# Transposing the normalised input by DMA instead of on TensorE

## Chip, cores and metric

One NeuronCore of a Trainium2 chip runs the whole program; all float32 inputs and the float32 output lie in HBM. The metric is device time in microseconds (us), the median of several runs. The cores of such a chip have five engines: TensorE (PE, matrix products into PSUM), VectorE (DVE), ScalarE (ACT), GpSimd (POOL) and SyncE (SP), which here only issues DMAs.

## What is computed

The input is x of shape (4, 2048, 512), four sequences. The reference, cut to what matters:

```python
xn  = layernorm(x)                                   # over 512 columns, no gain or bias
q,k,v = heads(xn @ Wq.T + bq), ...                   # 64 heads of 8
q,k = softmax(exp(beta) * q), softmax(exp(beta) * k) # within a head
num = einsum(q, cumsum(k v)); den = sum(q * cumsum(k))   # causal linear attention
attn = (num / den) @ Wo.T + bo
ffn  = fp8_round(clip(xn / input_scale)) @ (weight_fp8 * weight_scale).T + bias
out  = x + attn + ffn
```

## The kernel before

The 2048 positions are cut into 64 steps of 32 positions; a step takes them from all four sequences, so it is a tile of 128 rows (partitions) by 512 columns. Step i is spread over several bodies: body i of every engine holds the projections of step i, the causal scores, the state and the attention sums of step i - 1, and the output projection, the fp8 part and the final sum of step i - 2. Each engine has its own instruction stream with its own `body(i)`; nothing but hand-placed semaphore waits orders them. What an engine is given later in its own stream can't overtake what stands ahead of it.

The input of step i + 1 is prepared within body i. In the kernel before:

- DVE normalises it near the start of its body (`normalise`, L556, writes xn, L561), after a_n of step i - 2 and before `shift` of step i takes k_max and k_shift from the K bank (L594, L598).
- PE transposes xn late in its body (`input_transpose`, L834 to L839, four float32 128x128 transposes into the PSUM bank t_ps), between the output projection (L817 to L819) and the state part of the attention sums (L941).
- ACT reads t_ps twice (`high_input`, L409 to L418): xh, the float16 high part, and y, the value to be rounded to fp8. It does so behind q_heads (L464).
- DVE takes the low part, xl = t_ps - xh (`low_input`, L570), then y_exp and y_magic (`magic`, L575, L580), all after o_sb of step i - 2 (L704), then vp of step i (L713), which waits for PE's V projection of step i, and last xq, the clipped rounded value (`quantise`, L588).
- POOL adds and takes away y_magic (`rounding`, L357, L361), which rounds, and then adds the bias to the residual x_res (L373).

PE's body starts with the K projection of step i (`project`, L806 to L810: per 128-row chunk xh by w_hi, xh by w_lo, xl by w_hi, twelve matmuls), which waits for xh and xl of that step and for the bank's seed. Its V projection waits for o_sb of step i - 2, for it uses the same bank; it ends the body together with the last attention sums (L955).

The reciprocal standard deviations are made for two steps at a time, only in bodies with an even i: DVE computes the two variances and a first guess (`variances`, L542 to L554) near the end of its body, behind `statistics` of step i + 3; POOL refines the guess with three Newton rounds (`root`, L330 to L351, twelve small dependent operations). In POOL's body of an even i `root(i + 2)` stands first, ahead of `rounding(i + 1)` (L365 to L368). DVE's `quantise(i + 1)` waits for that rounding. Below, an even body that has these is called a root step, the others plain steps.

SP's body loads x of step i + 4 once xn of step i + 1 has been made, stores o_sb of step i - 2 and loads x_res of step i. DVE, ACT and POOL take all bodies from 4 to 59 in a loop of four; so did SP.

Of the kernel before, what the change touches and what calls it, by code (L numbers as in the profile page):

```python
# [31 lines left out]
P = 128  # L32
# [87 lines left out]
def build(nc, x, wq, bq, wk, bk, wv, bv, wo, bo, beta, wf, bf, in_scale, w_scale, const, out):  # L120
# [3 lines left out]
    with ExitStack() as ctx:  # L124
# [46 lines left out]
        xn = sb("xn", [P, DM])  # L171
        xh = sb("xh", [P, 2, KC, P], F16)
        xl = sb("xl", [P, 2, KC, P], F16)
        y = sb("y", [P, DM])
# [66 lines left out]
        newton_steps = sem("newton_steps")  # L241
        xn_ready, xT_done, xh_ready, xl_ready = sem("xn_ready"), sem("xT_done"), sem("xh_ready"), sem("xl_ready")
        y_ready, yexp_ready, magic_ready = sem("y_ready"), sem("yexp_ready"), sem("magic_ready")
# [47 lines left out]
        @block.sync  # L291
        def _(sp):
            def load_x(t):
                if t.after(SLOTS):
                    sp.wait_ge(xn_ready, (t - SLOTS + 1).n)
                sp.dma_start(x_in[:, t.slot, :], x_t[t.n]).then_inc(x_loaded[t.slot], 16)

            def body(i):
                if (i + SLOTS).exists():
                    load_x(i + SLOTS)  # L300
                t = i - 2
                if t.exists():
                    sp.wait_ge(o_ready, (t + 1).n)
                    sp.dma_start(out_t[t.n], o_sb[:, t.parity, :]).then_inc(stored[t.parity], 16)
                if i.exists():
                    sp.dma_start(x_res[:, i.parity, :], x_t[i.n]).then_inc(r_loaded[i.parity], 16)

            for n, s in enumerate((beta, in_scale, w_scale)):
                sp.dma_start(scal[:, n:n + 1], s.rearrange("(a n) -> a n", a=1).to_broadcast([P, 1]))\
                    .then_inc(m_loaded, 16)  # L310
            for t in range(PAIR):
                load_x(Step(0, t))
            sp.dma_start(cst[:, :], const).then_inc(c_loaded, 16)
            for m in turn:
                sp.dma_start(w_nat[m][:, :, :], weights[m].rearrange("(c p) d -> p c d", p=P))\
                    .then_inc(w_loaded[m], 16)
            for t in range(PAIR, SLOTS):
                load_x(Step(0, t))
            iterations(sp, body)
            for n in range(2):  # L320
                sp.wait_ge(stored[n], 16 * (STEPS // 2))
# [3 lines left out]
        def _(pool):  # L325
# [4 lines left out]
            def root(t):  # L330
# [5 lines left out]
                for n in range(NEWTON):  # L336
# [14 lines left out]
                    r = nxt  # L351

            def rounding(t):

                pool.wait_ge(y_ready, (t + 1).n)
                pool.wait_ge(magic_ready, (t + 1).n)
                gp.tensor_tensor(y_sum[:, :], y[:, :], y_magic[:, :], ALU.add).then_inc(ysum_ready, 1)  # L357
                pool.wait_ge(ysum_ready, (t + 1).n)
                if t.after(1):
                    pool.wait_ge(xq_ready, t.n)  # L360
                gp.tensor_tensor(y_round[:, :], y_sum[:, :], y_magic[:, :], ALU.subtract)\  # L361
                    .then_inc(yround_ready, 1)

            def body(i):
                if i.parity == 0 and (i + PAIR).exists():  # L365
                    root(i + PAIR)
                if (i + 1).exists():
                    rounding(i + 1)  # L368
                t = i - 1
# [5 lines left out]

            root(Step(0, 0))
            rounding(Step(0, 0))
            pool.wait_ge(amax_ready, 3)
# [24 lines left out]
        def _(act):  # L403
# [5 lines left out]
            def high_input(t):  # L409

                act.wait_ge(xT_done, (t + 1).n)
                if t.after(2):
                    act.wait_ge(v_done, (t - 1).n)
                sc.activation(flat(xh[:, t.parity]), t_ps[:, :], ACT.Copy).then_inc(xh_ready, 1)
                if t.after(1):
                    act.wait_ge(ysum_ready, t.n)
                    act.wait_ge(magic_ready, t.n)
                sc.activation(y[:, :], t_ps[:, :], ACT.Copy, scale=in_inv[:, :]).then_inc(y_ready, 1)  # L418

            def body(i, last_weights=None, fold=False):  # L420
                t = i - 1
                if t.exists():
# [4 lines left out]
                    for b in range(SEQS):  # L427
                        last = sc.activation(v_seqs[:, t.parity, :, b, :], vp[:, t.parity, :, :],  # L428
                                             ACT.Copy, scale=seq_mask[:, b:b + 1])
                    last.then_inc(vseqs_ready, 1)  # L430
                if i.exists():
                    act.wait_ge(kshift_ready, (i + 1).n)
# [18 lines left out]
                if i.exists():  # L451
# [14 lines left out]
                    last.then_inc(qheads_ready, 1)  # L466
                if (i + 1).exists():
                    high_input(i + 1)
                t = i - 1
# [50 lines left out]
        def _(dve):  # L520
# [35 lines left out]
            def normalise(t):  # L556

                dve.wait_ge(rstd_ready, (t + PAIR).half)
                if t.after(1):
                    dve.wait_ge(xT_done, t.n)  # L560
                v.tensor_scalar(xn[:, :], x_in[:, t.slot, :], mv[:, t.slot, 0:1],  # L561
                                rstd[:, t.slot:t.slot + 1], ALU.subtract, ALU.mult).then_inc(xn_ready, 1)

            def low_input(t):

                dve.wait_ge(xh_ready, (t + 1).n)
                dve.wait_ge(y_ready, (t + 1).n)
                if t.after(2):
                    dve.wait_ge(v_done, (t - 1).n)
                v.tensor_tensor(flat(xl[:, t.parity]), t_ps[:, :], flat(xh[:, t.parity]), ALU.subtract)\  # L570
                    .then_inc(xl_ready, 1)

            def magic(t):

                v.tensor_scalar(y_exp[:, :].bitcast(I32), y[:, :].bitcast(I32), EXPONENT, None,  # L575
                                ALU.bitwise_and).then_inc(yexp_ready, 1)
# [6 lines left out]
            def quantise(t):  # L583

                dve.wait_ge(yround_ready, (t + 1).n)
                if t.after(SLOTS):
                    dve.wait_ge(f_done, (t - SLOTS + 1).n)
                v.tensor_scalar(flat(xq[:, t.slot]), y_round[:, :], FP8_MAX, -FP8_MAX, ALU.min, ALU.max)\  # L588
                    .then_inc(xq_ready, 1)
# [38 lines left out]
            def body(i, last_weights=None, fold=False):  # L628
# [38 lines left out]
                if i.exists():  # L667
# [4 lines left out]
                    if i.after(2):  # L672
# [4 lines left out]
                        .then_inc(kT_ready, 1)  # L677
                    shift(i, q_ps, q_done, q_max, qmax_ready, q_shift, qshift_ready, qe_ready)
                t = i - 1
                if t.exists():  # L680
# [26 lines left out]
                if t.exists():  # L707
                    low_input(t)
                    magic(t)
                if i.exists():  # L710
# [4 lines left out]
                        .then_inc(vp_ready, 1)  # L715
                if t.exists():
                    quantise(t)

# [40 lines left out]
            largest(MQ)  # L759
            low_input(Step(0, 0))  # L760
            magic(Step(0, 0))
# [33 lines left out]
        def _(pe):  # L795
# [7 lines left out]
            def project(bank, t, m, seeded):  # L803

                for c in range(KC):
                    mm(bank[:, :], xh[:, t.parity, c, :], w_hi[:, m, c, :], start=(c == 0 and not seeded),  # L806
                       stop=False, skip_group_check=seeded)
                    mm(bank[:, :], xh[:, t.parity, c, :], w_lo[:, m, c, :], start=False, stop=False,  # L808
                       skip_group_check=seeded)
                    last = mm(bank[:, :], xl[:, t.parity, c, :], w_hi[:, m, c, :], start=False,  # L810
                              stop=(c == KC - 1), skip_group_check=seeded)
# [21 lines left out]

            def input_transpose(t):  # L834

                pe.wait_ge(xn_ready, (t + 1).n)
                for c in range(KC):
                    last = transpose(t_ps[:, P * c:P * (c + 1)], xn[:, P * c:P * (c + 1)], ident)
                last.then_inc(xT_done, 1)  # L839

            def body(i, low_part=True, last_weights=None, fold=False):
                if i.exists():
                    pe.wait_ge(xh_ready, (i + 1).n)
                    pe.wait_ge(xl_ready, (i + 1).n)
                    pe.wait_ge(kseed_ready, (i + 1).n)
# [10 lines left out]
                if t.exists():  # L856
                    pe.wait_ge(an_ready, (t + 1).n)
                    if i.exists():
                        pe.wait_ge(y_ready, (i + 1).n)
                    for b in range(SEQS):  # L860
# [3 lines left out]
                if fold:  # L864
                    pe.wait_ge(bias_ready, 3)
                    pe.wait_ge(y_ready, (i + 1).n)
                    for j in range(J):
# [22 lines left out]
                if t.exists():  # L890
                    pe.wait_ge(xq_ready, (t + 1).n)
                    if (t + 1).exists():
# [30 lines left out]
                if (i + 1).exists():  # L923
                    if fold:
                        pe.wait_ge(bvl_ready, 1)
                    else:
                        pe.wait_ge(xl_ready, (i + 1).n)
                        pe.wait_ge(y_ready, (i + 1).n)
                    input_transpose(i + 1)
                t = i - 1  # L930
# [48 lines left out]
            pe.wait_ge(c_loaded, 16)  # L979
            input_transpose(Step(0, 0))  # L980
            for m in (MK, MQ, MV):
# [45 lines left out]
```

## Time and profile before

| | us |
|---|---|
| runs of the kernel before | 1460.99, 1455.46, 1458.12 (median 1458.12) |
| the profiled execution | 1454.77 |
| its span, first to last instruction | 1452.9 |

| engine | busy us | share of the span |
|---|---|---|
| PE | 1328.5 | 91% |
| DVE | 1130.3 | 78% |
| ACT | 704.8 | 49% |
| POOL | 333.6 | 23% |

Busy time counts each instruction from its start to its modelled end; matmuls overlap, so PE's share is not a share of its peak. The DMA engines moved 61.83 MB, a mean of 43 GB/s. The granted TensorE clock was 0.985 of full speed over the span. The steady part runs from about 105 us to the end.

### The profile page before, as it was taken

How to read it: one execution, taken by the hardware profiler on the slowest of the kernel's cores; microseconds unless marked ns; L12 is line 12 of the kernel's file. 1: busy time of each engine (PE TensorE's matmuls, PEld its weight loads, DVE VectorE, ACT ScalarE, POOL GpSimd, SP SyncE). 2: the span in 40 equal slices, each digit the busy share in tenths (PEclk: the TensorE clock that was granted, in tenths of full speed). 3: DMA queues.
4: the chain of work that ended last, by engine and by line, in shares of the span. 5: the costliest groups of instructions: out<-in, count | busy, mean ns of one | idle time of the engine just before them, and what ended most of it. 6: DMA issues, size and time to landing. Idle time of an engine off the chain costs nothing.

```text
span 1452.9 us, 81228 instructions
## 1 busy us (share of the span) xinstructions
PE 1328.5 (91%) x36578; PEld 827.2 (57%) x36578; DVE 1130.3 (78%) x2095; ACT 704.8 (49%) x1241; POOL 333.6 (23%) x588
## 2 busy tenths in 40 slices
PE   1679999999999999999999999999999999999996
PEld 1345655655565555565556556556565655555664
DVE  3667877877787787787788778788778877877873
ACT  0554455545545544554554544555455455445542
POOL 1122222122222212212212222221222222122120
PEclk9699999999999999999999999999999999999999
DMA  7001111111111111111111111111111111111011
GB/s 216 25 10 28 45 47 33 39 46 40 33 46 46 30 42 47 33 39 47 36 36 46 43 30 46 47 34 38 47 40 32 46 46 31 41 46 34 24 33 33
DMA packets 29583, 61.83 MB, mean 43 GB/s; under 512 B 1377, under 2 KB 1505, under 8 KB 29281
## 3 DMA queue, kind: packets, MB, share of 16 engines
q1 hardware_dynamic: 28560, 55.67, 12.7%
q8 instruction: 291, 4.77, 1.4%
q10 hardware_dynamic: 720, 1.31, 0.4%
q14 instruction: 12, 0.09, 0.0%
HBM read 40.20 MB, written 16.78 MB: 39 GB/s over the span
## 4 chain that ended last, share of the span: by engine, by line
PE 33%; DVE 24%; issue 24%; POOL 11%; ACT 5%; DMA 1%; POOLq 1%; DVEq 0%; SPq 0%; ACTq 0%
PE s_ps L829 7%; POOL y_sum L357 3%; DVE st_step L612 3%; POOL y_round L361 3%; DVE att L623 3%; PE a_ps L955 2%; PE a_ps L915 2%; PE k_ps L806 2%; PE vo_ps L897 2%; DVE st_masked L606 2%; PE vo_ps L806 2%; PE k_ps L808 2%; PE k_ps L810 2%; DVE stats L536 2%; PE vo_ps L808 1%
## 5 line engine op out<-in xcount | busy, mean ns | idle before, releaser
L428 ACT ACTIVATE v_seqs<-vp,cst 128x576 f32<-128x576 f32 x256 | 184.8, 799 | 185.7 <-DVE vp L713 185.7
L829 PE MATMUL s_ps<-q_heads,kT 32*32 32x128 f32 x8192 | 249.7, 269 | 0.0
L829 PEld LDWEIGHTS s_ps<-q_heads,kT 32*32 32x32 f32 x8192 | 215.3, 105 | 53.7 <-issue 53.6
L357 POOL TENSOR_TENSOR y_sum<-y,y_magic 128x512 f32<-128x512 f32 x64 | 81.7, 1276 | 524.9 <-DVE y_magic L580 524.9
L464 ACT ACTIVATE q_heads<-qT,cst 128x512 f32<-128x512 f32 x256 | 164.1, 713 | 38.8 <-DVE qT L687 38.8
L623 DVE TENSOR_TENSOR att<-s_ps,cst 128x512 f32<-128x512 f32 x256 | 163.8, 681 | 0.2 <-PE s_ps L829 0.2
L455 ACT ACTIVATE q_e<-q_shift,q_exp_scale 128x512 f32<-128x512 f32 x64 | 46.3, 723 | 242.0 <-DVE q_shift L598 242.0
L588 DVE TENSOR_SCALAR xq<-y_round 128x512 f16<-128x512 f32 x64 | 92.0, 1437 | 80.4 <-POOL y_round L361 80.1
L436 ACT ACTIVATE k_e<-k_shift,k_exp_scale 128x512 f32<-128x512 f32 x64 | 46.3, 724 | 192.8 <-DVE k_shift L598 192.8
L806 PE MATMUL vo_ps<-w_hi,xh 128*128 128x512 f16 x256 | 97.7, 382 | 31.4 <-DVE o_sb L704 30.4
L713 DVE TENSOR_TENSOR vp<-vo_ps,vp 128x512 f32<-128x512 f32 x64 | 44.3, 692 | 102.6 <-PE vo_ps L810 102.6
L343 POOL TENSOR_TENSOR newton<-guess 128x2 f32<-128x2 f32 x32 | 6.2, 195 | 476.8 <-DVE guess L553 470.0
L806 PE MATMUL k_ps<-w_hi,xh 128*128 128x512 f16 x256 | 99.4, 388 | 12.2 <-issue 8.3
L941 PE MATMUL a_ps<-st_seqs,q_heads 128*32 128x36 f32 x8192 | 88.5, 201 | 20.0 <-issue 19.3
L817 PE MATMUL vo_ps<-w_hi,ah 128*128 128x512 f16 x260 | 99.5, 383 | 0.8 <-issue 0.8
L818 PE MATMUL vo_ps<-w_lo,ah 128*128 128x512 f16 x260 | 98.8, 380 | 0.7 <-issue 0.7
L808 PE MATMUL k_ps<-w_lo,xh 128*128 128x512 f16 x256 | 98.7, 385 | 0.6 <-issue 0.6
L819 PE MATMUL vo_ps<-w_hi,al 128*128 128x512 f16 x260 | 98.7, 380 | 0.2 <-issue 0.2
L810 PE MATMUL k_ps<-w_hi,xl 128*128 128x512 f16 x256 | 98.4, 384 | 0.0
L941 PEld LDWEIGHTS a_ps<-st_seqs,q_heads 128*32 128x32 f32 x8192 | 78.7, 109 | 33.6 <-issue 33.0
L955 PEld LDWEIGHTS a_ps<-v_seqs,att 128*32 128x32 f32 x8192 | 78.0, 109 | 33.7 <-issue 33.6
L808 PE MATMUL vo_ps<-w_lo,xh 128*128 128x512 f16 x256 | 97.0, 379 | 0.0
(138 smaller groups left out, 2648.5 us busy)
## 6 DMA issues: line engine op xcount, KB each, us to landing
x_in<-L_attn_x SPq DMA_DIRECT2D x64, 256.0 KB
x_res<-L_attn_x SPq DMA_DIRECT2D x64, 256.0 KB
out<-o_sb SPq DMA_DIRECT2D x64, 256.0 KB
w_own<-L_attn_Wk SPq DMA_DIRECT2D x1, 1024.0 KB, 12.4
w_own<-L_attn_Wq SPq DMA_DIRECT2D x1, 1024.0 KB, 14.4
w_own<-L_attn_Wv SPq DMA_DIRECT2D x1, 1024.0 KB, 16.2
att<-L_ffn_weight_fp SPq DMA_DIRECT2D x1, 1024.0 KB, 17.8
v_seqs<-L_attn_Wo SPq DMA_DIRECT2D x1, 1024.0 KB, 15.3
```

Of the source, the lines that this page charges most:

```text
L357: gp.tensor_tensor(y_sum[:, :], y[:, :], y_magic[:, :], ALU.add).then_inc(ysum_ready, 1)
L428: last = sc.activation(v_seqs[:, t.parity, :, b, :], vp[:, t.parity, :, :], ACT.Copy, scale=seq_mask[:, b:b + 1])
L464: last = sc.activation(q_heads[:, i.parity, :, j, :], qT[:, :, :], ACT.Copy, scale=head_mask[:, j:j + 1])
L623: v.tensor_tensor(att[:, 4 * c:4 * c + 4, :, :].rearrange("p g j s -> p (g j) s"), s_ps[:, DM * (c % 2):DM * (c % 2 + 1)].rearrange("p (h ...
L806: mm(bank[:, :], xh[:, t.parity, c, :], w_hi[:, m, c, :], start=(c == 0 and not seeded), stop=False, skip_group_check=seeded)
L808: mm(bank[:, :], xh[:, t.parity, c, :], w_lo[:, m, c, :], start=False, stop=False, skip_group_check=seeded)
L810: last = mm(bank[:, :], xl[:, t.parity, c, :], w_hi[:, m, c, :], start=False, stop=(c == KC - 1), skip_group_check=seeded)
L817: mm(vo_ps[:, :], ah[:, j, :], w_hi[:, MO, j, :], start=(j == 0 and not rest), stop=False)
L818: mm(vo_ps[:, :], ah[:, j, :], w_lo[:, MO, j, :], start=False, stop=False)
L829: last = mm(s_ps[rows, DM * (c % 2) + P * gg:DM * (c % 2) + P * (gg + 1)], kT[rows, t.parity, g, :], q_heads[rows, t.parity, g, :, :], sta ...
L941: mm(a_ps[TOK * j:TOK * (j + 1), a_col(g):a_col(g) + GW], q_heads[:, t.parity, g, j, :], st_seqs[:, t.parity, g, :, :], start=(g % (G // 2 ...
L955: last = mm(a_ps[TOK * j:TOK * (j + 1), a_col(g):a_col(g) + GW], att[:, g, j, :], v_seqs[:, t.parity, J * g + j, :, :], start=False, stop= ...
```

## The change

xn is no longer transposed on PE. ACT writes the float16 high part of xn in the natural layout into one half of a new tile x_split, POOL writes the low part into the other half (`low_input` is now POOL's), and SP transposes both halves with one DMA (`dma_start_transpose`, 128x1024 float16) into xT, of which there are two. y and the fp8 rounding are in the natural layout too; DVE writes xq_rows (one buffer), and SP transposes it (128x512 float16) into xq.

Order on the engines: ACT's `high_input(i + 1)` moves to the front of the body, behind v_seqs and ahead of k_e. DVE's `magic(i + 1)` moves ahead of the second pair of score masks (L623), `quantise(i + 1)` ahead of vp, and `low_input` leaves DVE. POOL runs `low_input(i + 1)` between `root(i + 2)` and `rounding(i + 1)`. SP issues both transposes behind the load of x and ahead of the store of o_sb and the load of x_res; its bodies are written out instead of looped. PE waits for x_turned in place of xh and xl, and for xq_turned in place of xq. The transposes of a_n now wait for al of the step before (L659) in place of y. The diff, cut:

```diff
 SP
+            def turn_x(t):
+                sp.wait_ge(xl_ready, (t + 1).n)
+                if t.after(2):
+                    sp.wait_ge(v_done, (t - 1).n)
+                sp.dma_start_transpose(xT[:, t.parity].rearrange("p h c s -> p (h c) s"),
+                                       x_split[:, :, :].rearrange("p h d -> p (h d)")).then_inc(x_turned, 16)
+                sp.wait_ge(xq_ready, (t + 1).n)
+                if t.after(SLOTS):
+                    sp.wait_ge(f_done, (t - SLOTS + 1).n)
+                sp.dma_start_transpose(xq[:, t.slot, :, :], xq_rows[:, :]).then_inc(xq_turned, 16)
             def body(i):
                 if (i + SLOTS).exists():
                     load_x(i + SLOTS)
+                if (i + 1).exists():
+                    turn_x(i + 1)
 POOL
+            def low_input(t):
+                pool.wait_ge(xh_ready, (t + 1).n)
+                gp.tensor_tensor(x_split[:, 1, :], xn[:, :], x_split[:, 0, :], ALU.subtract)\
+                    .then_inc(xl_ready, 1)
                 if i.parity == 0 and (i + PAIR).exists():
                     root(i + PAIR)
                 if (i + 1).exists():
+                    low_input(i + 1)
                     rounding(i + 1)
 ACT, high_input(t), now behind v_seqs in body(i)
-                act.wait_ge(xT_done, (t + 1).n)
-                if t.after(2):
-                    act.wait_ge(v_done, (t - 1).n)
-                sc.activation(flat(xh[:, t.parity]), t_ps[:, :], ACT.Copy).then_inc(xh_ready, 1)
+                act.wait_ge(xn_ready, (t + 1).n)
+                if t.after(1):
+                    act.wait_ge(x_turned, t.n * 16)
+                sc.activation(x_split[:, 0, :], xn[:, :], ACT.Copy).then_inc(xh_ready, 1)
-                sc.activation(y[:, :], t_ps[:, :], ACT.Copy, scale=in_inv[:, :]).then_inc(y_ready, 1)
+                sc.activation(y[:, :], xn[:, :], ACT.Copy, scale=in_inv[:, :]).then_inc(y_ready, 1)
 DVE
             def normalise(t):
-                    dve.wait_ge(xT_done, t.n)
+                    dve.wait_ge(xl_ready, t.n)
+                    dve.wait_ge(y_ready, t.n)
                     shift(i, q_ps, q_done, q_max, qmax_ready, q_shift, qshift_ready, qe_ready)
+                if (i + 1).exists():
+                    magic(i + 1)
                 t = i + 1
                 if t.exists():
-                    low_input(t)
-                    magic(t)
+                    quantise(t)
                 if i.exists():
                     dve.wait_ge(v_done, (i + 1).n)
                     ...                               # vp
-                if t.exists():
-                    quantise(t)
 DVE, quantise(t)
-                if t.after(SLOTS):
-                    dve.wait_ge(f_done, (t - SLOTS + 1).n)
-                v.tensor_scalar(flat(xq[:, t.slot]), y_round[:, :], FP8_MAX, -FP8_MAX, ALU.min, ALU.max)\
+                if t.after(1):
+                    dve.wait_ge(xq_turned, t.n * 16)
+                v.tensor_scalar(xq_rows[:, :], y_round[:, :], FP8_MAX, -FP8_MAX, ALU.min, ALU.max)\
 PE
-                    pe.wait_ge(xh_ready, (i + 1).n)
-                    pe.wait_ge(xl_ready, (i + 1).n)
+                    pe.wait_ge(x_turned, (i + 1).n * 16)
-                    if i.exists():
-                        pe.wait_ge(y_ready, (i + 1).n)
+                    if t.after(1):
+                        pe.wait_ge(al_ready, t.n)
-                    pe.wait_ge(xq_ready, (t + 1).n)
+                    pe.wait_ge(xq_turned, (t + 1).n * 16)
-                if (i + 1).exists():
-                    ...
-                    input_transpose(i + 1)
```

## Rows read from the trace of the kernel before

**Rows 1.** The page: busy time of each engine, and its share of the span.
```profile
PE 1328.5 (91%) x36578; PEld 827.2 (57%) x36578; DVE 1130.3 (78%) x2095; ACT 704.8 (49%) x1241; POOL 333.6 (23%) x588
```
**Rows 2.** Timeline of DVE: start, length, line, operation [idle before, releaser].
```profile
704.93 0.68 DVE L594 TENSOR_REDUCE k_max<-k_ps 128x64 f32<-128x512 f32 x1
...
717.81 0.17 DVE L553 TENSOR_SCALAR guess<-shifted 128x2 int32<-128x2 int32 x1
717.98 0.75 DVE L704 SCALAR_TENSOR_TENSOR o_sb<-vo_ps,out_dn,x_res 128x512 f32<-128x512 f32 x1
...
721.59 0.69 DVE L713 TENSOR_TENSOR vp<-vo_ps,vp 128x512 f32<-128x512 f32 x1 [1.47 <-PE vo_ps L810]
724.18 1.49 DVE L588 TENSOR_SCALAR xq<-y_round 128x512 f16<-128x512 f32 x1 [1.89 <-POOL y_round L361]
725.59 0.56 DVE L635 RECIPROCAL den_rec<-a_ps 128x32 f32<-128x32 f32 x2
...
727.30 0.69 DVE L594 TENSOR_REDUCE k_max<-k_ps 128x64 f32<-128x512 f32 x1
...
739.31 0.75 DVE L704 SCALAR_TENSOR_TENSOR o_sb<-vo_ps,out_dn,x_res 128x512 f32<-128x512 f32 x1
...
747.46 0.68 DVE L594 TENSOR_REDUCE k_max<-k_ps 128x64 f32<-128x512 f32 x1
```
**Rows 3.** All of k_max in the trace: least, median, longest ns, first and last start.
```profile
L594 DVE TENSOR_REDUCE k_max<-k_ps x64: 681/686/694, 58.0 to 1407.8; 128x64 f32<-128x512 f32 x64
```
**Rows 4.** Timeline of POOL in the root step of Rows 2.
```profile
718.06 0.20 POOL L343 TENSOR_TENSOR newton<-guess 128x2 f32<-128x2 f32 x1 [15.04 <-DVE guess L553]
...
721.36 0.20 POOL L349 TENSOR_TENSOR rstd<-newton 128x2 f32<-128x2 f32 x1
721.51 1.29 POOL L357 TENSOR_TENSOR y_sum<-y,y_magic 128x512 f32<-128x512 f32 x1
722.88 1.27 POOL L361 TENSOR_TENSOR y_round<-y_sum,y_magic 128x512 f32<-128x512 f32 x1
724.10 1.28 POOL L373 TENSOR_TENSOR x_res<-x_res,bias 128x512 f32<-128x512 f32 x1
```
**Rows 5.** Timeline of PE over the same two steps; only first matmuls of groups.
```profile
716.55 0.60 PE L838 MATMUL t_ps<-cst,xn 128*128 128x128 f32 x4
717.08 1.31 PE L941 MATMUL a_ps<-st_seqs,q_heads 128*32 128x36 f32 x128
...
722.73 0.39 PE L806 MATMUL k_ps<-w_hi,xh 128*128 128x512 f16 x1
...
725.42 1.95 PE L829 MATMUL s_ps<-q_heads,kT 32*32 32x128 f32 x64
...
740.12 0.39 PE L806 MATMUL vo_ps<-w_hi,xh 128*128 128x512 f16 x1 [1.08 <-DVE o_sb L704]
...
744.05 0.39 PE L806 MATMUL k_ps<-w_hi,xh 128*128 128x512 f16 x1
```
**Rows 6.** Groups by line: busy us, mean ns, idle before and its releaser.
```profile
L580 DVE TENSOR_SCALAR y_magic<-y_exp 128x512 f32<-128x512 f32 x64 | 27.3, 427 | 2.2
L575 DVE TENSOR_SCALAR y_exp<-y 128x512 int32<-128x512 int32 x64 | 26.8, 419 | 0.0
L343 POOL TENSOR_TENSOR newton<-guess 128x2 f32<-128x2 f32 x32 | 6.2, 195 | 476.8 <-DVE guess L553 470.0 <-issue 6.8
```
**Rows 7.** DMA issues of the start: size, median us from issue to landing.
```profile
scal<-L_attn_beta SPq DMA_DIRECT2D x1, 0.5 KB, 2.6
bias<-L_attn_bq ACTq DMA_DIRECT2D x1, 256.0 KB, 4.5
w_own<-L_attn_Wk SPq DMA_DIRECT2D x1, 1024.0 KB, 12.4
```
**Rows 8.** Stretches of PE in body 1: length, busy, granted clock; and its timeline.
```profile
74.00:76.00 2.00, 0.00 (x0) 0.70 0.00 0
```
```profile
78.47 0.58 PE L806 MATMUL k_ps<-w_hi,xh 128*128 128x512 f16 x1 [7.46 <-issue]
...
82.69 1.95 PE L829 MATMUL s_ps<-q_heads,kT 32*32 32x128 f32 x64
```

More of the change, by code:

```diff
@@ L171, in build @@
         xn = sb("xn", [P, DM])
-        xh = sb("xh", [P, 2, KC, P], F16)
-        xl = sb("xl", [P, 2, KC, P], F16)
+        x_split = sb("x_split", [P, 2, DM], F16)
+        xT = sb("xT", [P, 2, 2, KC, P], F16)
+        xq_rows = sb("xq_rows", [P, DM], F16)
         y = sb("y", [P, DM])
@@ L241, in build @@
         newton_steps = sem("newton_steps")
-        xn_ready, xT_done, xh_ready, xl_ready = sem("xn_ready"), sem("xT_done"), sem("xh_ready"), sem("xl_ready")
+        xn_ready, xh_ready, xl_ready = sem("xn_ready"), sem("xh_ready"), sem("xl_ready")
+        x_turned, xq_turned = sem("x_turned"), sem("xq_turned")
         y_ready, yexp_ready, magic_ready = sem("y_ready"), sem("yexp_ready"), sem("magic_ready")
@@ L318, in _ @@
                 load_x(Step(0, t))
-            iterations(sp, body)
+            turn_x(Step(0, 0))
+            for i in range(STEPS + 2):
+                body(Step(0, i))
             for n in range(2):
@@ L376, in _ @@
             root(Step(0, 0))
+            low_input(Step(0, 0))
             rounding(Step(0, 0))
@@ L430, in body @@
                     last.then_inc(vseqs_ready, 1)
+                if (i + 1).exists():
+                    high_input(i + 1)
                 if i.exists():
@@ L466, in body @@
                     last.then_inc(qheads_ready, 1)
-                if (i + 1).exists():
-                    high_input(i + 1)
                 t = i - 1
@@ L559, in normalise, with magic @@
                 if t.after(1):
-                    dve.wait_ge(xT_done, t.n)
+                    dve.wait_ge(xl_ready, t.n)
+                    dve.wait_ge(y_ready, t.n)
                 v.tensor_scalar(xn[:, :], x_in[:, t.slot, :], mv[:, t.slot, 0:1],
                                 rstd[:, t.slot:t.slot + 1], ALU.subtract, ALU.mult).then_inc(xn_ready, 1)
-            def low_input(t):
-                dve.wait_ge(xh_ready, (t + 1).n)
+            def magic(t):
                 dve.wait_ge(y_ready, (t + 1).n)
[L568 to L573, printed above, removed]
                 v.tensor_scalar(y_exp[:, :].bitcast(I32), y[:, :].bitcast(I32), EXPONENT, None,
@@ L678, in body @@
                     shift(i, q_ps, q_done, q_max, qmax_ready, q_shift, qshift_ready, qe_ready)
+                if (i + 1).exists():
+                    magic(i + 1)
                 t = i - 1
@@ L759, in _ @@
             largest(MQ)
-            low_input(Step(0, 0))
             magic(Step(0, 0))
@@ L805, in project @@
                 for c in range(KC):
-                    mm(bank[:, :], xh[:, t.parity, c, :], w_hi[:, m, c, :], start=(c == 0 and not seeded),
+                    mm(bank[:, :], xT[:, t.parity, 0, c, :], w_hi[:, m, c, :], start=(c == 0 and not seeded),
                        stop=False, skip_group_check=seeded)
-                    mm(bank[:, :], xh[:, t.parity, c, :], w_lo[:, m, c, :], start=False, stop=False,
+                    mm(bank[:, :], xT[:, t.parity, 0, c, :], w_lo[:, m, c, :], start=False, stop=False,
                        skip_group_check=seeded)
-                    last = mm(bank[:, :], xl[:, t.parity, c, :], w_hi[:, m, c, :], start=False,
+                    last = mm(bank[:, :], xT[:, t.parity, 1, c, :], w_hi[:, m, c, :], start=False,
                               stop=(c == KC - 1), skip_group_check=seeded)
@@ L832, in scores @@
                 last.then_inc(scores_done, 1)
[L834 to L839, printed above, removed]
             def body(i, low_part=True, last_weights=None, fold=False):
                 if i.exists():
-                    pe.wait_ge(xh_ready, (i + 1).n)
-                    pe.wait_ge(xl_ready, (i + 1).n)
+                    pe.wait_ge(x_turned, (i + 1).n * 16)
                     pe.wait_ge(kseed_ready, (i + 1).n)
@@ L857, in body @@
                     pe.wait_ge(an_ready, (t + 1).n)
-                    if i.exists():
-                        pe.wait_ge(y_ready, (i + 1).n)
+                    if t.after(1):
+                        pe.wait_ge(al_ready, t.n)
+                    else:
+                        pe.wait_ge(bvl_ready, 1)
                     for b in range(SEQS):
@@ L865, in body @@
                     pe.wait_ge(bias_ready, 3)
-                    pe.wait_ge(y_ready, (i + 1).n)
                     for j in range(J):
@@ L979, in _ @@
             pe.wait_ge(c_loaded, 16)
-            input_transpose(Step(0, 0))
             for m in (MK, MQ, MV):
```

6 lines of the change are left out of this document (removed).

## The prediction

> **What bounds the kernel now.** The page's busy times [rows 1] make PE look like the bound at 91%. Two views next to each other correct that. The DVE timeline gives the pace: k_max, one per step, starts at 704.93, 727.30 and 747.46 [rows 2], so a root step takes 22.37 us and a plain step 20.16 us, 42.53 for the pair. Over the trace, 63 intervals from 58.0 to 1407.8 us make 21.4 us each [rows 3], the same half pair, so what holds for one pair holds for the kernel. Newton rounds start 32 times [rows 6]; one is ahead of the loop, so 31 bodies are root steps.
>
> Why is a root step 2.2 us longer? DVE's guess ends at 717.98, POOL's Newton chain runs from 718.06 to 721.56, y_sum and y_round follow from 721.51 to 724.15 [rows 4], and DVE's xq waits 1.89 us for y_round; only then come den_rec and the next k_max [rows 2]. So the chain guess, Newton, rounding, xq sets the length of a root step. PE starts its next K projection at 722.73 and is done by 725.42 [rows 5], 1.9 us before DVE takes k_max: PE is not late there. In the plain step DVE runs nearly without a stop from k_max (727.30) to the end of o_sb (740.06), V starts at 740.12 having waited 1.08 us for it [rows 5], and the period closes through xq again. There both engines are near their limits.
>
> One more thing is in these rows. xq takes 1.49 us, y_magic, the same kind of operation, 0.43 [rows 6]. xq starts at 724.18, just behind the start of POOL's x_res (724.10 to 725.38) [rows 4]; it ends just after it.
>
> **The change, part by part.**
>
> *PE* loses four transposes: 716.55 to 717.08, 0.53 us a step [rows 5], 34 us over 64 steps. This is worth something only where PE is the late one, which it isn't in a root step.
>
> *DVE* loses xl (0.60 us), which lay in the wait for the V projection, where there is 1.47 us of idle time besides. That gain is nothing. y_exp and y_magic (0.42 + 0.43 = 0.85 us [rows 6]) come out of that same cover and go into the stretch between k_max and o_sb, which has no slack. So o_sb, and in a root step the guess too, come 0.85 us later. xq moves into the wait for V. In a plain step that takes it off the path, and away from x_res: it should take about 0.43.
>
> *Plain step after:* k_max to the end of o_sb 12.76 + 0.85 = 13.61. Then 0.06, then V, the last attention sums and K: 740.12 to 744.05 is 3.93, and K is 2.69 long (722.73 to 725.42) [rows 5]. Sum 20.3 against 20.16. The xq path gave room but o_sb, V, K close in its place: no gain, + 0.15 us.
>
> *Root step after,* counted from k_max (704.93 = 0). POOL's order is root(i + 2), low_input(i + 1), rounding(i + 1). So the low part of the next step's input, which DVE used to make at 718.65 without asking POOL, now stands behind the Newton chain:
> - guess ends at 13.05 + 0.85 = 13.90;
> - Newton 3.50 + 0.08 (717.98 to 721.56): 17.48;
> - low_input on POOL, two inputs 128x512, nearest row y_sum, 1.29 [rows 4]: 18.8;
> - the DMA transpose of 256 KB, issue to landing: D, below;
> - K of the next step 2.69, then k_max.
>
> D is in no row: no DMA transposes here. The lower bound is the 0.5 KB load, 2.6 us from issue to landing, the upper the 1 MB load of 12.4 us (which had two loads beside it) [rows 7]. Nearest in size is the first bias row, 256 KB, 4.5 us; I take that. With 0.1 us for the waits on both sides K starts at 23.4 and ends at 26.1.
>
> The Trainium skill has two rules that disagree here. "Advanced Engine Details and Errata", section X-Bar Transpose (TRN2), says transpose DMAs are as fast as regular ones, which goes with the 4.5 us row. "VectorE: DVE Perf Modes", The three transpose paths, gives 1309 ns for one 128x128 block by DMA against 390 on TensorE, which speaks against the change; one after the other, eight blocks would be an estimate of 10.5 us, and the total about 1810. No row decides between them.
>
> The clock. PE's last work before that K ends 13.90 + 0.75 (o_sb) + 0.06 + 3.93 = 18.65. So PE would be idle for 4.8 us in every root step. The trace has such a case in body 1: idle from about 71 us, the granted clock fell within 74 to 76 us, and the K projection after it took 78.47 to 82.69 = 4.22 us in place of 2.69 [rows 8]. That is 1.2 for 2.4 GHz through most of it: + 1.53. K ends at 27.6, and the root step is 27.6 against 22.37: + 5.25.
>
> *The other path of a root step,* which K hides by then: rounding behind low_input ends at 18.8 + 2.64 = 21.45; xq beside x_res as now 1.41 (724.18 to 725.59); vp, now behind xq, 0.69; den_rec to k_max 1.71 [rows 2]. Sum 25.3. So a root step can't be under 25.3 whatever D is: quantise now stands ahead of vp and takes it along. This is the floor: + 2.9.
>
> *The rest at nothing.* In a plain step low_input follows xn and xh at the start of the body, some 6 us after PE's K start, and K of the next step is 20 us behind K: even D = 12.4 is hidden, if by 1 or 2 us only. ACT's two operations move ahead of k_e; ACT waits for k_shift there now, and its early place is free as long as v_seqs (started by vp) is out of the way, which holds where K is the late one. The transpose of xq has two bodies before PE reads it. SP waits for xq_ready in mid-body with the store of o_sb, the load of x_res and the next load of x behind it; the first two used to wait for o_sb, which ends 8 us earlier in a root step and 0.5 in a plain one, and x_res has a whole body until POOL adds it, the load of x four. If that cover went, a late x_res would hold o_sb and so V, us for us. Body 0 has a root step too; I charge it like the others.
>
> **Sum.** 31 x 5.25 = 163, 31 x 0.15 = 5. On the profiled execution's 1454.8 that gives 1623 us. It lies 3.4 us (0.2%) under the median of the runs, which I leave inside the range.
>
> **Rivals.**
>
> 1. *The clock stays up.* PE idles under 2 us at a time in the steady part now and keeps its clock; at 4.8 us the fall in body 1 speaks for a loss. Without it: 31 x 3.7 + 5 = 120, 1575 us.
> 2. *Rounding decides, not the transpose.* If D is under 3.7 us, K ends before 25.3 and the xq, vp path closes the step: 31 x 2.9 + 5 = 95, 1550 us. For it: the 0.5 KB load lands in 2.6 us, and the source is on the chip. Against: 256 KB took 4.5.
> 3. *Slow transposes.* With D = 12.4, K ends at 18.8 + 12.5 + 2.69 + 1.53 = 35.5: 31 x 13.1 + 5 = 412, 1867 us. For it: nothing in the trace moves two-byte elements from one partition to another, so the row I took may be of the wrong kind. Against: the DMA engines are almost idle in this trace (43 GB/s).
> 4. *Faster.* The mechanism: xq under the V projection, and four transposes fewer. It decides if neither path behind Newton is late, that is if K's path and xq's path of a root step both stay under 22.37, for which D would have to be under 0.9 us and the rounding 2.9 us earlier. Then a root step would close like a plain one, with 0.6 us for variances: 20.9, and the pair 41.2 in place of 42.5: 31 x 1.3 = 40, 1414 us. Against it stand POOL's order and the rows of the Newton chain.
>
> **Chances.** Forecast (root step closed by a transpose of 3.7 to 8 us, clock lost) 0.42; the same with the clock kept 0.15; rounding decides 0.15; slow transposes, over 8 us, 0.19; faster 0.05; the parts cancel within 0.5% (what a measurement of this kernel can tell from no change) 0.04. Faster by over 0.5% 0.05, same 0.04, slower 0.91. The range: the low end is the floor of the root step, 1550. The far end of D, 1867, stands for the last tenth of the chances; I stop at 1810, where D would be 10.5, so that about 2 in 10 lie outside in all.
>
> **What the profile of after would show.** Right: k_max intervals that alternate near 20.3 and 25 to 28; K's first matmul in root steps waiting for x_turned, released by the DMA; POOL's low part starting as rstd ends in root steps, but right behind xh in plain ones; granted clock under 1.00 in the steady part. xq near 0.43 us in plain steps. Rival 2: vp waits, K doesn't. Rival 3: PE waits for the DMA in plain steps too, or for 10 us and more in root steps. Wrong altogether: root steps no longer than 22.4, which would mean that POOL's low part doesn't stand behind Newton.

## The result: 19% slower, and both kinds of step are longer

| | kernel before | changed kernel |
|---|---|---|
| median of the runs, us | 1457.4 | 1732.0 |
| lowest to highest | 1455.5 to 1461.0 | 1723.9 to 1740.5 |
| span of the profiled execution | 1452.9 | 1732.3 |
| mean granted clock | 0.985 | 0.924 |
| root step, mean of 30 (steps 2 to 60) | 22.5 | 25.7 |
| plain step, mean of 29 (steps 3 to 59) | 20.3 | 26.3 |

The ratio is 1.189, 95% interval 1.184 to 1.193. The step lengths are differences between successive starts of DVE's k_max, from the timeline over the whole trace. The forecast was 1623 us in a range of 1550 to 1810: the sign and the range held. But the pair of steps was to be 27.6 + 20.3 and came out as 25.7 + 26.3: by the step lengths 31 x 6.0 = 186 us of the loss come from the plain steps, which the forecast had charged with 5, and 31 x 3.2 = 99 from the root steps, charged with 163.

The page of the changed kernel (busy us, share of the span; then the time by the chain that ended last):

```profile
PE 1395.9 (81%) x36322; PEld 821.5 (47%) x36322; DVE 1058.5 (61%) x2031; ACT 708.5 (41%) x1241; POOL 392.7 (23%) x652
...
issue 36%; PE 31%; DVE 13%; POOL 9%; DMA 6%; ACT 3%; POOLq 1%; DVEq 0%; SPq 0%; ACTq 0%
```

Against [rows 1], the shares of PE, DVE and ACT are lower and POOL's is the same: no engine has become the bound, all of them wait. "issue" is time in which the engine waited for nothing that the profile shows. Who waits for what on PE (total us, times, longest):

```profile
PE k_ps L822 <- DMA xT<-x_split: 106.6, 31, 14.7
PE a_ps L924 <- issue: 101.2, 27, 7.2
```

The first row was forecast: 31 waits, one in each root step. The second was not. It sits in the middle of the state matmuls (L924); of its 27 waits 24 are over 1.5 us, and all of those lie in plain steps. Over the whole trace PE waits 143 us for "issue", in the kernel before 39.

**A root step** (timeline of DVE, with those of POOL, SP and PE; it answers to [rows 2] and [rows 4]):

```profile
789.97 0.69 DVE L612 TENSOR_REDUCE k_max<-k_ps 128x64 f32<-128x512 f32 x1 [0.79 <-PE k_ps L826]
...
803.39 0.17 DVE L578 TENSOR_SCALAR guess<-shifted 128x2 int32<-128x2 int32 x1
803.56 0.75 DVE L724 SCALAR_TENSOR_TENSOR o_sb<-vo_ps,out_dn,x_res 128x512 f32<-128x512 f32 x1
810.82 1.38 DVE L606 TENSOR_SCALAR xq_rows<-y_round 128x512 f16<-128x512 f32 x1 [6.51 <-POOL y_round L384]
812.12 0.68 DVE L732 TENSOR_TENSOR vp<-vo_ps,vp 128x512 f32<-128x512 f32 x1
```
```profile
806.73 0.19 POOL L366 TENSOR_TENSOR rstd<-newton 128x2 f32<-128x2 f32 x1
806.88 1.17 POOL L373 TENSOR_TENSOR x_split<-xn,x_split 128x512 f16<-128x512 f32 x1
```
```profile
808.08 1.28 SPq L304 DMA_TRANSPOSE xT<-x_split  x1
```
```profile
810.89 0.46 PE L822 MATMUL k_ps<-w_hi,xT 128*128 128x512 f16 x1 [2.51 <-DMA xT<-x_split]
...
815.27 1.95 PE L845 MATMUL s_ps<-q_heads,kT 32*32 32x128 f32 x64
```

The low part stands right behind the last Newton operation, as forecast. The transpose goes out at 808.08 and K starts at 810.89: 2.8 us. K takes 4.38 us, from 810.89 to 815.27, instead of the 2.69 of [rows 5]. Through most of it the granted clock is 0.50 (the second row below, 1.2 in place of 2.4 GHz):

```profile
810.00:812.00 2.00, 1.11 (x4) 0.77 0.17 37
812.00:814.00 2.00, 2.00 (x6) 0.50 0.38 70
```

**The plain step behind it** (timeline of PE, then of SP, then of DVE):

```profile
823.17 1.28 PE L924 MATMUL a_ps<-vp,k_e 32*32 32x36 f32 x111
829.88 0.46 PE L924 MATMUL a_ps<-vp,k_e 32*32 32x36 f32 x17 [5.43 <-issue]
```
```profile
812.23 1.86 SPq L309 DMA_TRANSPOSE xq<-xq_rows  x1
814.14 0.59 SPq L319 DMA_DIRECT2D out<-o_sb  x1
814.77 0.56 SPq L321 DMA_DIRECT2D x_res<-L_attn_x  x1
815.38 0.54 SPq L298 DMA_DIRECT2D x_in<-L_attn_x  x1
817.47 6.12 SPq L304 DMA_TRANSPOSE xT<-x_split  x1
```
```profile
836.11 0.42 DVE L606 TENSOR_SCALAR xq_rows<-y_round 128x512 f16<-128x512 f32 x1
```

PE stops after 111 of 128 matmuls of one group that share their waits; the other 17 come 5.4 us later. No operand can be missing there. The stall costs more than its 5.4 us: behind it PE runs at half clock, and the twelve matmuls of the output projection (L833 to L835) take from 830.28 to 835.28, 5.0 us, where the same twelve took 2.6 us in the kernel before.

```profile
830.00:832.00 2.00, 2.00 (x22) 0.50 0.00 0
```

Averaged over the 29 plain steps, PE's "issue" waits are 4.5 us a step (0.5 before), and the time that the lower clock withheld (the length of a stretch times the share not granted) is 2.0 us (none before). The two rises together, 4.0 + 2.0, are as large as the growth of the plain step, 6.0 us.

In the DMA view the queue "instruction" (291 packets with 4.77 MB in the kernel before, 16 KB each) is absent while three plain copies and the transpose are under way, and has its next packet just as that ends (first answer: 814 to 827 us, second: 827 to 829):

```profile
DMA  1000153100222222239922222222222222561117
...
q1 hardware_dynamic: 1147, 0.97, 82.3%
```
```profile
q1 hardware_dynamic: 363, 0.08, 19.6%
q8 instruction: 1, 0.02, 3.4%
```

The long run of twos in the first line, in tenths of the 16 DMA engines, is the copies: they keep about a quarter of the engines busy. The landing of this transpose took 12.0 us after its issue, in place of the 2.8 us in the root step.

The nines in that line are not traffic. A packet's whole time is counted where it starts, and this is the stretch from 820 to 821 us by itself:

```profile
q1 hardware_dynamic: 301, 0.15, 746.5%
```

The 301 packets that start in this one microsecond take 7.5 times the time of all 16 engines. Single packets of the trace say why: 17 packets of the transpose, 256 bytes each, start between 820.15 and 820.50 and last 6.4 to 6.7 us, where the median of such a packet is 0.02 us. All 17 end at 826.83 to 826.87, just behind the last packet of the copies (826.56). The next load of the "instruction" queue runs from 827.29 to 828.38, and PE goes on at 829.88.

### The profile page after: what moved, and what is told of

The parts are those of the page before. It is cut to its first block, busy times and chain, and to the rows that moved or that the text cites. A ratio compares the mean times of both kernels' runs of the same rounds, so it can differ in the third digit from the quotient of the medians.

```text
span 1732.3 us, 80448 instructions
## 1 busy us (share of the span) xinstructions
PE 1395.9 (81%) x36322; PEld 821.5 (47%) x36322; DVE 1058.5 (61%) x2031; ACT 708.5 (41%) x1241; POOL 392.7 (23%) x652
## 2 busy tenths in 40 slices
DMA packets 131981, 86.98 MB, mean 50 GB/s; under 512 B 103776, under 2 KB 103904, under 8 KB 131680
## 4 chain that ended last, share of the span: by engine, by line
issue 36%; PE 31%; DVE 13%; POOL 9%; DMA 6%; ACT 3%; POOLq 1%; DVEq 0%; SPq 0%; ACTq 0%
DMA xT<-x_split 5%; PE s_ps L845 5%; PE k_ps L822 3%; PE k_ps L826 3%; PE k_ps L824 3%; POOL x_split L373 2%; PE a_ps L924 2%; PE a_ps L957 2%; POOL y_sum L380 2%; PE a_ps L943 1%; DVE st_step L630 1%; PE vo_ps L906 1%; PE vo_ps L833 1%; PE vo_ps L822 1%; PE vo_ps L834 1%
## 5 line engine op out<-in xcount | busy, mean ns | idle before, releaser
L822 PE MATMUL k_ps<-w_hi,xT 128*128 128x512 f16 x256 | 116.4, 455 | 113.7 <-DMA xT<-x_split 106.6
L606 DVE TENSOR_SCALAR xq_rows<-y_round 128x512 f16<-128x512 f32 x64 | 55.6, 869 | 202.1 <-POOL y_round L384 202.1
L924 PE MATMUL a_ps<-vp,k_e 32*32 32x36 f32 x8064 | 90.4, 198 | 101.3 <-issue 101.2
L924 PEld LDWEIGHTS a_ps<-vp,k_e 32*32 32x32 f32 x8064 | 79.4, 106 | 131.4 <-issue 131.1
L822 PE MATMUL vo_ps<-w_hi,xT 128*128 128x512 f16 x256 | 101.9, 398 | 38.5 <-DVE o_sb L724 34.5
L500 ACT ACTIVATE st_seqs<-st_run,cst 128x144 f32<-128x144 f32 x252 | 84.3, 410 | 89.2 <-DVE st_run L635 89.1
L826 PE MATMUL k_ps<-w_hi,xT 128*128 128x512 f16 x256 | 116.2, 454 | 1.4 <-issue 1.4
L824 PE MATMUL k_ps<-w_lo,xT 128*128 128x512 f16 x256 | 116.3, 454 | 0.0
L833 PE MATMUL vo_ps<-w_hi,ah 128*128 128x512 f16 x260 | 111.8, 430 | 0.0
L835 PE MATMUL vo_ps<-w_hi,al 128*128 128x512 f16 x260 | 110.1, 423 | 0.0
L624 DVE TENSOR_TENSOR st_masked<-a_ps,cst 128x288 f32<-128x288 f32 x126 | 50.5, 440 | 94.5 <-PE a_ps L924 94.3
L373 POOL TENSOR_TENSOR x_split<-xn,x_split 128x512 f16<-128x512 f32 x64 | 74.4, 1162 | 145.3 <-ACT x_split L439 145.3
```

What stands on the lines that cost most here:

```text
L822: mm(bank[:, :], xT[:, t.parity, 0, c, :], w_hi[:, m, c, :], start=(c == 0 and not seeded), stop=False, skip_group_check=seeded)
L824: mm(bank[:, :], xT[:, t.parity, 0, c, :], w_lo[:, m, c, :], start=False, stop=False, skip_group_check=seeded)
L826: last = mm(bank[:, :], xT[:, t.parity, 1, c, :], w_hi[:, m, c, :], start=False, stop=(c == KC - 1), skip_group_check=seeded)
L833: mm(vo_ps[:, :], ah[:, j, :], w_hi[:, MO, j, :], start=(j == 0 and not rest), stop=False)
L835: last = mm(vo_ps[:, :], al[:, j, :], w_hi[:, MO, j, :], start=False, stop=(j == J - 1))
L924: last = mm(a_ps[rows, col:col + J * VW], k_e[rows, t.parity, TOK * g:TOK * (g + 1)], vp[rows, t.parity, J * g:J * (g + 1), :], start=True ...
```

## Experiments

Theory N: the low part behind the Newton chain, as in the forecast. Theory F, formed from the rows above: a transpose that is queued behind copies which occupy few DMA engines starts on the free engines, and its packets hold them until the last ones join; PE's instruction loads wait with them, and PE, whose stream is written out and must be loaded all the time, runs dry.

**e1: POOL's order.**

```diff
-                if i.parity == 0 and (i + PAIR).exists():
-                    root(i + PAIR)
                 if (i + 1).exists():
                     low_input(i + 1)
                     rounding(i + 1)
+                if i.parity == 0 and (i + PAIR).exists():
+                    root(i + PAIR)
```

> The changed kernel, but POOL makes the low part and the rounding of the next step ahead of the Newton rounds instead of behind them. Two theories. N (Newton order, the one of the prediction, holds most of the loss): root steps fall from 25.7 us to about 21, plain ones stay, 31 x 4.7 = 146 us less, about 1586 us. F (instruction fetch: a DMA transpose queued behind the plain copies, which run on few DMA engines, keeps the other engines waiting for each other, and PE's instruction loads with them): now the transpose comes right behind the copies in root steps too, so these get the stall of the plain ones, and both take 25 to 27 us: 1690 to 1760 us.

Measured 1492.8 us, ratio 1.026 (1.024 to 1.028); root steps 21.6, plain steps 22.0. Neither expectation was met: N's half came true (root steps 21.6), and the plain steps fell by 4.3 us with them. Timeline of SP, one step:

```profile
819.04 1.19 SPq L309 DMA_TRANSPOSE xq<-xq_rows  x1
820.29 0.58 SPq L319 DMA_DIRECT2D out<-o_sb  x1
820.91 0.55 SPq L321 DMA_DIRECT2D x_res<-L_attn_x  x1
821.51 0.55 SPq L298 DMA_DIRECT2D x_in<-L_attn_x  x1
826.90 2.62 SPq L304 DMA_TRANSPOSE xT<-x_split  x1
```

The big transpose goes out 5.4 us behind the last copy, where it was 2.1 us in the changed kernel. So I had the premise of F's expectation wrong: without the late low part the copies have a head start. The bunch of transfers behind a root step is a consequence of the Newton order. Transpose packets are still held here, for up to 4.6 us (7.7 in the changed kernel), but no two instruction loads are more than 9.1 us apart (17.8 there). PE's issue waits at the state matmuls are down from 101 to 24 us, not gone.

**e2: the copies cut by sequence,** for x, x_res and out alike; the counts that wait for them go from 16 to 64.

```diff
-                sp.dma_start(x_in[:, t.slot, :], x_t[t.n]).then_inc(x_loaded[t.slot], 16)
+                for b in range(SEQS):
+                    sp.dma_start(x_in[TOK * b:TOK * (b + 1), t.slot, :], x_t[t.n][b])\
+                        .then_inc(x_loaded[t.slot], 16)
```

> The changed kernel, but each plain copy of 128x512 (x, x_res, out) is cut in four of 32 rows, one for each sequence, so that it may use more than the quarter of the DMA engines that the trace shows busy. F: the transpose no longer waits, PE's instruction loads come in time, plain steps fall from 26.3 to about 20.4 us, root steps stay at 25.7: about 1550 us. If the transposes by themselves starve the loads, or if N is all: within 20 us of 1732.

Measured 1592.0 us, ratio 1.095 (1.091 to 1.098); root steps 25.5, plain steps 21.8. F's expectation in sign and place: root steps untouched, plain steps 4.5 us shorter, though not the 5.9 expected. The wait at the state matmuls, 101.2 us in the changed kernel, is down to:

```profile
PE a_ps L930 <- issue: 8.0, 14, 1.1
```

The waits of K for x_turned in the root steps are as they were (104.7 us against 106.6).

**e3: both edits.**

> Both edits. F and N together: root steps about 20.9, plain ones about 20.4, some 1415 us, which would be under the kernel before (1457). If the transposes starve PE without the copies: over 1580 us.

Measured 1441.9 us, ratio 0.991 (0.988 to 0.993); both kinds of step 21.2. Faster than the kernel before, but 27 us short of what was expected.

**e4: plain copies in place of the transposes.**

```diff
-                sp.dma_start_transpose(xT[:, t.parity].rearrange("p h c s -> p (h c) s"),
-                                       x_split[:, :, :].rearrange("p h d -> p (h d)")).then_inc(x_turned, 16)
+                sp.dma_start(xT[:, t.parity].rearrange("p h c s -> p (h c s)"),
+                             x_split[:, :, :].rearrange("p h d -> p (h d)")).then_inc(x_turned, 16)
```

> The changed kernel with both DMA transposes replaced by plain DMA copies of the same bytes to the same place, 128 rows each; the transposing is left out. F: no engine waits for another in a plain copy, PE's instruction loads get through, plain steps about 20.4, root steps about 25.4 or less: about 1545 us. If the traffic of 0.38 MB a step, or the new waits and SP's order of issue, are the cause: 1700 us or more.

Measured 1593.1 us, ratio 1.093 (1.089 to 1.098); root steps 25.1, plain steps 22.1. Same bytes, same waits, same place in the queue, and 139 us less: the volume of traffic and SP's new order are out as the main cause. The plain copies also make fewer packets (48,013 in all against 131,981), so that e4 alone leaves their number open; e9 and e10 below keep the packets of the transposes. The root step is hardly shorter, because a plain copy of that size takes nearly as long to land there (median 3.0 us, the transpose 3.4).

**e5: the kernel before, with a transpose added.**

```diff
                 if i.exists():
                     sp.dma_start(x_res[:, i.parity, :], x_t[i.n]).then_inc(r_loaded[i.parity], 16)
+                if i.exists() and i.after(2):
+                    if i.n == 2:
+                        sp.wait_ge(fold_ready, 1)
+                    if i.after(3):
+                        sp.wait_ge(spared, (i - 2).n * 16)
+                    sp.dma_start_transpose(spare[:, i.parity].rearrange("p h c s -> p (h c) s"),
+                                           w_hi[:, MK, 0:2, :].rearrange("p c d -> p (c d)")).then_inc(spared, 16)
```

> The kernel before, with one thing added: in every step SP issues a DMA transpose of 128x1024 float16 of w_hi into a tile nobody reads, behind the load of x_res and ahead of the next load of x; no compute engine waits for it (SP's stream is written out, as in the changed kernel). F: PE's instruction loads are held up in root and plain steps alike, 2 to 6 us a step, 1580 to 1800 us, with idle time of PE that waits for issue. N, or any theory in which the loss comes from waits of compute engines: within 10 us of 1457.

Measured 1780.0 us, ratio 1.226 (1.221 to 1.231). This is the strongest case: no compute engine waits for the result, no order on a compute engine is changed, and the kernel loses more than by the whole change. PE's "issue" waits are 267 us in all, in root and plain steps. The longest group of them, and the landing of the added transpose:

```profile
PE s_ps L840 <- issue: 163.1, 35, 6.2
```
```profile
spare<-w_hi SPq DMA_TRANSPOSE x62, 11.3
```

The order of events is the same each time. From 110 us on PE has 46 such waits of over 2 us here. 43 of them end 1.2 to 1.7 us behind the end of an instruction load, which itself ends 1.0 to 1.6 us behind held transpose packets. In the changed kernel it is 24 of 32.

**e10: the same, once the copy ahead has landed.**

```diff
+                    sp.wait_ge(r_loaded[i.parity], (i + 2).half * 16)
                     sp.dma_start_transpose(spare[:, i.parity].rearrange("p h c s -> p (h c) s"),
```

> e5, but SP waits until the load of x_res has landed before it issues the added transpose. F: a transpose on free engines takes its 3 us and holds nobody: 1455 to 1475 us against 1780 of e5. If transposes as such starve PE's instruction loads: 1550 us or more.

Measured 1461.1 us, ratio 1.004 (1.002 to 1.006); the landing is 3.1 us, and plain steps are 20.4. One SP wait takes 319 us away. No transpose packet lasts over 1.5 us here, and PE's "issue" waits are 44 us in all. The 62 transposes on a free queue cost this kernel 5 us together.

```profile
spare<-w_hi SPq DMA_TRANSPOSE x62, 3.1
```

**e9: the same wait in the changed kernel,** for the load of x issued just before.

```diff
+                if t.after(1) and (t + 3).exists():
+                    sp.wait_ge(x_loaded[(t + 3).slot], (t + 3 + SLOTS).quarter * 16)
                 sp.dma_start_transpose(xT[:, t.parity].rearrange("p h c s -> p (h c) s"),
```

> The changed kernel, but SP waits until the load of x issued just before has landed ahead of the big transpose; the copies are cut as before. F (a transpose queued behind copies that run on a quarter of the engines holds the others): the queue is empty then, PE's loads aren't held, the transpose itself comes later by some 8 us in plain steps, which is hidden: as e2, 1580 to 1620 us. If what helped in e2 was only that the copies are finished sooner or smaller: no change, 1732.

Measured 1597.2 us, ratio 1.101 (1.097 to 1.105); root steps 25.5, plain steps 21.6. The copies are as large and as slow as before; only the transpose no longer stands behind them. So it is the queueing, not the size of the copies.

**e6: control, the kernel before with the copies cut.**

> The kernel before, with its plain copies cut in four as in e2 and nothing else. No DMA is waited for there in the steady part, and PE's loads aren't held up: within 10 us of 1457 by either theory. It is the control for e2 and e3.

Measured 1449.6 us, ratio 0.996 (0.994 to 0.998): 6 us of e2's and e3's gain may belong to the cutting alone.

**e8: Newton order in the kernel before,** the edit of e1 there.

> The kernel before with one edit: POOL rounds for the next step ahead of the Newton rounds instead of behind them. If the Newton chain is what makes a root step of the kernel before 2.2 us longer than a plain one, root steps fall from 22.5 to about 20.5 us: 31 x 2 = 62 less, about 1393 us, and this one edit is worth more than e3 is. If the Newton result itself is due just as early (it ends 1.3 us later than now, at about 0.6 us before DVE takes it), the gain is half or less: 1420 to 1455.

Measured 1461.8 us, ratio 1.005 (1.003 to 1.007); root steps 22.6. No gain at all, which neither side of the expectation had. Timeline of DVE:

```profile
810.71 0.43 DVE L588 TENSOR_SCALAR xq<-y_round 128x512 f16<-128x512 f32 x1 [0.65 <-POOL y_round L361]
...
813.96 1.47 DVE L561 TENSOR_SCALAR xn<-x_in,mv,rstd 128x512 f32<-128x512 f32 x1 [1.12 <-POOL rstd L349]
```

xq waits less (0.65 us in place of 1.89) and is short; but now xn waits 1.12 us for the Newton result and then runs beside POOL's x_res (1.47 us in place of 0.54). The wait has changed hands. In the changed kernel the same swap is worth 239 us for two reasons that are absent here: it takes the low part, and with it the transpose and K, out from behind the Newton chain (root steps 4.1 us shorter), and it lets the transpose go out longer after the copies (plain steps 4.3 us shorter).

**e7: y_exp and y_magic in a gap,** on top of e3.

```diff
                     mask_scores(t, 0)
                     mask_scores(t, 1)
+                if (i + 1).exists():
+                    magic(i + 1)
```

(and not ahead of the last two masks)

> e3, and DVE's y_exp and y_magic of the next step stand right behind the first two score masks, where DVE waits 0.6 us for ACT's ah in every step, and not ahead of the last two. If the stretch of DVE from k_max to o_sb closes both kinds of step in e3 (21.2 us each), 0.6 of their 0.85 us is covered: 20.6 us a step, about 1441 - 62 x 0.6 = 1404 us. If PE or its instruction loads close the step there, no change: 1441.

Measured 1424.6 us, ratio 0.980 (0.978 to 0.983); root steps 20.8, plain steps 21.0. Against e3 it is 17 us less, half of the 37 expected: the stretch of DVE was only part of what closes the step there. It is the best version that was run, 2.0% under the kernel before (interval 1.7 to 2.2).

## The prediction, point by point

*Where the change acts.* "k_max to k_max" as the pace, root and plain steps apart, and POOL's Newton chain as the hinge of a root step: right. A view by engine shares wouldn't have shown it, as PE was at 91% [rows 1] and lost its transposes without any gain.

*The root step, 27.6 forecast, 25.7 measured.* Counted from the k_max of the step shown (789.97), with the forecast in brackets: end of guess 13.6 (13.9), end of Newton 17.0 (17.5), end of low_input 18.1 (18.8), K starts 20.9 (23.4), K ends 25.3 (27.6). The chain and its order held link by link. The mis-sized term is D, taken from the 256 KB row of [rows 7] at 4.5, with 0.1 for the waits: it was 2.8, near the lower bound of 2.6 (over the root steps the median is 3.4, from 2.7 to 4.7). That row was a load from HBM. The clock term held in this step: K took 1.69 us longer, 1.53 was charged. PE had stood idle for 2.5 us before it, not the 4.8 forecast, and the clock fell all the same. But in 8 of the 30 root steps it did not fall, though PE stood idle there for 2.4 to 3.4 us too, and these steps are 24.1 to 24.7 us long.

*The floor, 25.3.* The path by xq and vp: y_round ends at 20.7 (21.45), k_max could have started at about 24.5. It is done 0.9 us before K's path. So rival 2's condition (D under 3.7) was met in D, and it still didn't decide here, because K was at half clock. The condition itself was wrong beside a forecast that charges the clock: 3.7 holds for K at full speed; with the 1.53 us of the clock in the sum it is 2.2. Where the clock stayed up, rival 2 came true: in those 8 root steps k_max follows xn with no more than 0.2 us of waiting. The forecast's own case, a D of 3.7 to 8 us with the clock lost, was not met in most steps; that 25.7 is near 27.6 is the chain being right and D being too long.

*Rival 3.* With D = 12.4 in root steps it was to be 1867 us; D was 2.7 to 4.7 there. By the 1309 ns a block of "VectorE: DVE Perf Modes" in the Trainium skill (The three transpose paths), eight blocks one after the other would be an estimate of 10.5 us; eight blocks landed in 2.8 us here. The rule of "Advanced Engine Details and Errata" in the Trainium skill (X-Bar Transpose (TRN2)), transposes as fast as regular DMAs, agrees with e4, where the plain copy landed in 3.0 us against 3.4 and the root step changed by 0.6 us.

*The plain step, 20.3 forecast, 26.3 measured: this is the step that failed.* The sentence was "the rest at nothing ... even D = 12.4 is hidden". The landing was hidden, at 12.0 us even: PE never waited for x_turned there. What I named as cover was time until the data is needed. What I left out is who else uses the DMA engines meanwhile. The kernel before already had the signs: an "instruction" queue in the profile page's list of DMA queues, 291 packets of 4.77 MB in all, and a PE stream of 73 thousand instructions that is written out. A stall of those loads has no semaphore, so no argument from waits finds it. e2, e4 and e9 take most of it from plain steps by three different edits (140, 139, 135 us), and e5 and e10 make it and take it away without any of the change. The forecast also charged the clock to root steps alone; in plain steps it withheld 2.0 us as well.

*The two errors had opposite signs:* root steps 31 x 1.9 = 59 us too long, plain steps 31 x 6.0 = 186 us too short. The total was within 7% by partly cancelling. That is luck, and shouldn't be read as a sizing that was right.

*xq.* 0.42 us in plain steps, as forecast, and 1.38 in root steps beside x_res.

*Rival 4, faster.* Its mechanism is real: with both waits gone (e3) the kernel is 0.9% faster than before, with the y chain in a gap (e7) 2.0%. Its price was 1414 us; e7 reached 1425. What is left in e7 is the end of the step, where vp, den_rec and k_max each wait for PE. PE's issue waits are 35 us in all there, no more than the 39 of the kernel before.

## What stays open

That an instruction load waits behind held transpose packets is shown by the order of events (packets held, released, load, PE goes on), by e5 and by e10; on which DMA engine the load stood is not, for the trace does not tell which engine a packet used. Nor was it measured how long a load may be held before PE runs out: in e1 packets are held too, and PE hardly stops. It wasn't tried whether the copies, issued by ACT on its own queue, would still hold the transposes. e5 loses 325 us where the plain steps of the changed kernel lose 186; there the stall comes in root and plain steps alike (26.4 and 26.2 us), but why it is that long in each wasn't split up. Why the clock fell in 22 root steps and not in the other 8, after idle times of much the same length, is open as well.

## To carry to other kernels

When a transfer is called hidden, ask two things: when its data is needed, and what else stands in the queues that it passes through, the loads of instructions among them. Look for the stall with no releaser ("issue") in the middle of a group of matmuls with one wait; here it was the mark of an engine that lacked instructions. And before moving work off a busy engine, see whose stream it joins and behind what: the low part cost DVE nothing where it was, and on POOL it stood behind the Newton chain, which ends last in a root step.

## What the chip showed that I had not expected

- A DMA transpose of 128x1024 float16 from SBUF to SBUF lands about 3 us after its issue on a free queue (median 3.1 in e10, 3.4 in the root steps of the changed kernel), and 11.3 (e5) to 11.4 us (plain steps) behind 128x512 float32 copies that keep a quarter of the DMA engines busy. Meanwhile single packets of it last up to 7.7 us, and loads of instructions wait. SP itself is held while issuing: 1.28 us against 6.12 in the steps shown.
- Copies of 128x512 float32 whose HBM side has four sequences as its outer dimension keep about a quarter of the engines busy. Cut by sequence, each 64 KB lands in about 2 us, and the transpose behind them in 2.7 us (e2, plain steps).
- The same swap of two pieces of work on one engine was worth 239 us in one kernel and -6 us in the other.
